# Where the gates of a mixture of experts are applied: on the combined outputs, or on the output tiles before they leave

## The chip, the cores and the metric

One core of a Trainium2 chip runs the kernel. The metric is the device time of one execution in microseconds (us); lower is better. TensorE (PE) multiplies, VectorE (DVE), ScalarE (ACT) and GpSimd (POOL) do the element work, SyncE (SP) issues most transfers. On-chip memory is SBUF; products land in PSUM, which has 8 banks (`PS[0]` to `PS[7]`).

## The reference

Three layers on 2,048 tokens of 128 numbers: a mixture of experts, a Mamba block (the mixer), and the same mixture of experts again.

```
x = x + 0.5 * moe(layernorm(x));  x = x + mamba(layernorm(x));  x = x + 0.5 * moe(layernorm(x))

moe: logits = xt @ Wr + br                      # 8 experts
     top 2 of 8 per token; gate = softmax over these two logits
     h = relu(xt @ W1[e] + b1[e])               # 128 -> 512
     y = h @ W2[e] + b2[e]                      # 512 -> 128
     out = sum over the token's two experts of gate * y
```

All is float32. Every token has two gates, with the factor 0.5 of the layer in them.

## The kernel before, in words

**Layout.** The 2,048 tokens lie as 16 tiles of 128 (`X`, 128 partitions x 16 x 128), in four groups of four tiles (the batches). Each token goes to two experts, so there are 4,096 pairs (token, choice), which fill 4,096 slots, sorted by expert: 32 tiles of 128 slots (`DENSE`). Since an expert's slots need not end with a tile, the experts work in 39 steps (`SLOT_TILES`), each on 128 slots from a computed start.

**The route** (`route`, VectorE, L1373 to L1442). From the two best logits of each token come the slot of each pair, and from the slot a pair of one-hot matrices: `onehot_a` (which tile) and `onehot_b` (which place in it, 32 blocks of 128x128 in 16-bit floats). 32 small products (L764) of `onehot_b` and `onehot_a` with the pair's number give for each slot the row to read and to write (`rows_in`, `rows_out`). `b_wide` is a helper for `onehot_b`, written by ScalarE, and free afterwards. Last in the route, VectorE works out the gates of each token (L1440 to L1442).

**The experts** (39 steps, an order written out by hand for each engine). GpSimd gathers 32 tiles of normed rows from memory (`XG`, a ring of 8: gather i waits until tile i-8 is turned), then scatters 32 tiles of outputs (`YS`, a ring of 12) to `y_rows`. It works in order, so the first scatter stands behind the last gather. TensorE at step s: first products `up(s+1)` (L793, 4 fp32 products, 8 passes, W1 x tile), transposes of arriving tiles (L778), transposes of output tiles that leave (L814), then second products `down(s)` (L805, 8 passes). VectorE at step s: half of the relu of s+1 (L1465), the copy of arrived tiles out of PSUM to `XT_all` (L1454), bias of step s (`add_bias`, L1475, into `YT_all`), and the copy of the second weights of step s+3 (`W2B`, L1484); the first three such copies stand ahead of step -2. ScalarE: the other half of the relu (L1121), copies of the first weights (`W1B`, L1111), and the copies of leaving output tiles out of bank 6 into the ring `YS` (L1133, two tiles in one instruction).

**The join.** When all scatters have landed, SyncE loads the outputs group by group (L370): for each token its two rows, `Y1` and `Y2`. Then X += gate1 * Y1 + gate2 * Y2. VectorE does it in one instruction for a tile and choice (L1507). After the first layer groups 1, 2 and part of 3 are done by ScalarE, which multiplies by the gate (`gated`, L1153), and GpSimd, which adds (L497); after the second, group 3 is. Statistics, square roots (on GpSimd, L501) and the normed rows `XN` of the mixer follow: group 0 and 3 by VectorE (`norm`, L1338), groups 1 and 2 by ScalarE (`apply`, L1000); TensorE waits for each group's rows in `time_project`.

What sets the order is each engine's own list, and semaphores; `wait_ge` stops an engine and all that is behind it on its list.

Of the kernel before, what the change touches and what calls it, by code (L numbers as in the profile page):

```python
# [14 lines left out]
P = 128  # L15
# [63 lines left out]
TURN_AT = (1, 2, 5, 3, 4)  # L79
LEAVE_STEP = [tiles[-1] + NE for tiles in LEAVES]  # L80
# [22 lines left out]
def macaron_block(nc, x, in_proj_w, conv_w, conv_b, dt_bias, A_log, D_skip, norm_w, out_proj_w,  # L103
                  ln_w, ln_b, Wr, br, W1, b1, W2, b2, out):
    ctx = ExitStack()
    with ctx:
# [66 lines left out]
        gate = sb("gate", [P, KTOP, NT])  # L173
# [20 lines left out]
        b_wide = sb("b_wide", [P, NG, P], F16)  # L194
        rows_out = sb("rows_out", [P, DENSE], I32)
# [110 lines left out]
        s_gated = sem("s_gated")  # L306
# [50 lines left out]
        def wait_xn(engine, g):  # L357

            if g in (1, 2):
                engine.wait_ge(s_xn[1], NT + g * NC)  # L360
            else:
                engine.wait_ge(s_xn[0], NC * (1 if g == 0 else 2))
# [11 lines left out]
        def _(sp_):  # L374
# [29 lines left out]
            for g in range(BATCH):  # L404
                if g < BATCH - 1:
                    sp_.wait_ge(s_comb, 2 + g + 1)
                else:
                    sp_.wait_ge(s_comb_pool, 4)
# [18 lines left out]
        def _(pool):  # L427
# [66 lines left out]
            def add_output(k, g_, gated):  # L494
                xb = X[:, g_ * NC:(g_ + 1) * NC, :]
                pool.wait_ge(s_gated, gated)
# [23 lines left out]

            def join_last():
                st.link(add_output(0, 3, 6))
                add_output(1, 3, 7).then_inc(s_comb_pool, 1)
# [116 lines left out]
            join_last()  # L640

        @block.tensor
        def _(pe):
# [109 lines left out]
            def experts(layer):  # L753
# [55 lines left out]
                def leave(m):  # L809
                    pe.wait_ge(s_ytw, B0 + min(LEAVES[m][-1] + NE, SLOT_TILES))  # L810
                    if L0 + m:
                        pe.wait_ge(s_ysc, L0 + m)
                    for k, i in enumerate(LEAVES[m]):
# [3 lines left out]

                for step in range(-2, SLOT_TILES):
                    if 0 <= step + 1 < SLOT_TILES:
# [174 lines left out]
        def _(act):  # L994
# [8 lines left out]
            def store(n, g):  # L1003
                act.wait_ge(s_xn[1], (n // 2) * (NT + 2 * NC) + (g + 1) * NC)
# [20 lines left out]
            def time_project(besides):  # L1025
                act.wait_ge(s_xnd, 16 * BATCH)
                turned(1, 0)
                besides(0)
                besides(1)
                act.wait_ge(s_rs, 2)  # L1030
                apply(1, range(NC, 2 * NC))
                turned(1, 1)
                act.wait_ge(s_rs, 3)
# [781 lines left out]
```

## Time and profile before

| | |
|---|---|
| median of 3 runs | 417.07 us (416.44 to 419.63) |
| profiled execution | 421.09 us |
| its span, first to last instruction | 419.3 us |
| TensorE busy | 330.8 us (79%) |
| VectorE busy | 269.0 us (64%) |
| ScalarE busy | 209.8 us (50%) |
| GpSimd busy | 220.7 us (53%) |

A profile is one execution with the hardware profiler on. PE is TensorE's multiplying, PEld its loading of weights; L793 is line 793 of the kernel. PEclk is the clock granted to TensorE, as a share of the full one. A row "idle before" says how long the engine stood still and whose work ended that. Starts of matmuls that follow each other are partly modelled: when TensorE is really slower than the record, one sees it only from the engines that wait for its results.

### The profile page before, as it was taken

The page shows a single profiled execution, that of the slowest core. Times are in us where ns is not written, and L with a number is a line of the kernel's source. Part 1 is how long each engine was busy: PE and PEld are TensorE (multiplying, and loading weights), DVE is VectorE, ACT ScalarE, POOL GpSimd, SP SyncE. Part 2 cuts the span into 40 slices and gives each one's busy share as a digit, 9 for nine tenths or more (in the row PEclk, how much of TensorE's full clock was granted, in tenths as well). Part 3 has the DMA queues.
Part 4 walks back from the last instruction along what each step waited for, and adds up shares of the span by engine and source line. Part 5 has one row for each costly group of instructions (what it writes and reads, how often), then busy time and mean ns, then how long its engine had stood idle before and what let it go on. Part 6 is the DMA issues. An engine that isn't in the chain of part 4 may idle for free.

```text
span 419.3 us, 8909 instructions
## 1 busy us (share of the span) xinstructions
PE 330.8 (79%) x2366; PEld 294.6 (70%) x2366; DVE 269.0 (64%) x920; ACT 209.8 (50%) x501; POOL 220.7 (53%) x263
## 2 busy tenths in 40 slices
PE   8784799986698198799999999749469998778800
PEld 7684799976697185567777779739459998767700
DVE  4883477753465178768788986899447775345416
ACT  3832456644464065736657573453245665455402
POOL 4026355566545177274656879651644556654512
PEclk9578899999899598899999999877899999899965
DMA  6791111111111410000000000010111111111154
GB/s 161 239 283 45 27 39 42 40 44 44 41 33 33 172 48 2 1 0 2 1 2 3 0 0 2 2 74 28 52 31 39 38 41 45 41 40 38 33 172 147
DMA packets 18674, 22.23 MB, mean 53 GB/s; under 512 B 4114, under 2 KB 13508, under 8 KB 18628
## 3 DMA queue, kind: packets, MB, share of 16 engines
q1 hardware_dynamic: 13092, 11.18, 8.9%
q0 software_dynamic: 4096, 8.40, 6.7%
q10 hardware_dynamic: 1440, 2.11, 1.4%
q8 instruction: 21, 0.34, 0.4%
q14 instruction: 25, 0.20, 0.2%
HBM read 14.33 MB, written 7.34 MB: 52 GB/s over the span
## 4 chain that ended last, share of the span: by engine, by line
PE 51%; DVE 11%; issue 9%; DMA 6%; SPq 6%; ACT 5%; POOL 4%; another core or an unknown queue 3%; DVEq 3%; ACTq 0%; POOLq 0%
PE PS L793 16%; PE PS L805 16%; SPq L401 3%; PE PS L842 3%; PE PS L849 3%; PE PS L896 2%; PE PS L814 2%; PE PS L778 2%; DMA YT_all<-y_rows 2%; SPq L395 2%; DMA y_rows<-YS,rows_out 2%; DVE X L1507 2%; POOL rs L501 2%; DVE YT_all L1475 1%
## 5 line engine op out<-in xcount | busy, mean ns | idle before, releaser
L479 POOL DMA_INDIRECT XG<-xn_rows,rows_in x64 | 62.1, 970 | 83.8 <-issue 35.7
L793 PE MATMUL PS<-XT_all,W1B 128*128 x624 | 90.1, 290 | 15.8 <-DVE XT_all L1454 8.0
L793 PEld LDWEIGHTS PS<-XT_all,W1B 128*128 128x128 f32 x624 | 80.3, 201 | 18.9 <-issue 18.2
L1121 ACT ACTIVATE H<-PS,W1B 128x128 f32<-128x128 f32 x156 | 48.7, 363 | 88.9 <-PE PS L793 60.7
L489 POOL DMA_INDIRECT y_rows<-YS,rows_out x64 | 62.3, 974 | 48.3 <-issue 18.9
L805 PE MATMUL PS<-H,W2B 128*128 128x128 f32 x624 | 85.3, 281 | 0.5 <-issue 0.5
L805 PEld LDWEIGHTS PS<-H,W2B 128*128 128x128 f32 x624 | 78.4, 197 | 0.9 <-issue 0.6
L1484 DVE COPY W2B<-W2S 128x513 f32 x78 | 35.5, 455 | 39.1 <-DVE YT_all L1475 26.6
L1111 ACT ACTIVATE W1B<-W1S 128x516 f32 x78 | 49.4, 633 | 21.7 <-issue 9.0
L1475 DVE TENSOR_SCALAR YT_all<-PS,W2B 128x128 f32 x78 | 27.2, 349 | 43.3 <-PE PS L805 25.8
L1465 DVE TENSOR_SCALAR H<-PS,W1B 128x128 f32<-128x128 f32 x156 | 46.9, 342 | 6.4 <-PE PS L793 3.8
L650 PE MATMUL PS<-ones 128*128 128x128 f32 x236 | 38.8, 338 | 9.7 <-DMA YT_all<-y_rows 8.6
L650 PEld LDWEIGHTS PS<-ones 128*128 128x128 f32 x236 | 37.5, 251 | 10.4 <-DMA YT_all<-y_rows 8.8
L1637 DVE SCALAR_TENSOR_TENSOR XT_all<-PS,cw,XT_all 128x509 f32<-128x509 f32 (+2 forms) x48 | 35.6, 744 | 3.9 <-ACT XT_all L1165 2.5
L814 PE MATMUL PS<-ident,YT_all 128*128 128x128 f32 x64 | 13.8, 286 | 20.3 <-DVE YT_all L1475 14.8
L540 POOL TENSOR_TENSOR mix<-eseg,gm 128x512 f32<-128x512 f32 x16 | 20.3, 1269 | 14.3 <-DVE gm L1659 14.3
L842 PE MATMUL PS<-XNT,WT 128*128 128x512 f32 x48 | 25.9, 630 | 0.3 <-ACT XNT L1010 0.3
L1507 DVE SCALAR_TENSOR_TENSOR X<-YT_all,gate,X 128x128 f32<-128x128 f32 x36 | 12.7, 419 | 19.2 <-DMA YT_all<-y_rows 19.1
L814 PEld LDWEIGHTS PS<-ident,YT_all 128*128 128x128 f32 x64 | 7.5, 141 | 23.2 <-DVE YT_all L1475 16.8
L1183 ACT ACTIVATE eseg<-PS 128x512 f32<-128x512 f32 x16 | 9.6, 597 | 26.4 <-PE PS L849 26.4
L531 POOL TENSOR_TENSOR seg_rhs<-upto,la 128x512 f32<-128x512 f32 x16 | 16.6, 1039 | 11.4 <-DVE la L1543 7.2
L1153 ACT ACTIVATE YT_all<-YT_all,gate 128x128 f32<-128x128 f32 x28 | 8.4, 388 | 22.5 <-DMA YT_all<-y_rows 22.5
(204 smaller groups left out, 556.0 us busy)
## 6 DMA issues: line engine op xcount, KB each, us to landing
YT_all<-y_rows SPq DMA_DIRECT2D x8, 512.0 KB, 5.1
W1S<-in_L_ffn_W SPq DMA_DIRECT2D x1, 2048.0 KB
W2S<-in_L_ffn_W SPq DMA_DIRECT2D x8, 256.0 KB
xn_rows<-XN ACTq DMA_DIRECT2D x8, 256.0 KB, 4.4
X<-in_L_attn_x SPq DMA_DIRECT2D x4, 256.0 KB, 4.7
XG<-xn_rows,rows_in POOLq DMA_INDIRECT x64
y_rows<-YS,rows_out POOLq DMA_INDIRECT x64
out_x<-X SPq DMA_DIRECT2D x4, 256.0 KB, 2.3
```

What stands on the lines that cost most here:

```text
L479: g.indirect_dma_start(out=XG[:, u, :], out_offset=None, in_=xn_dram, in_offset=bass.IndirectOffsetOnAxis(ap=rows_in[:, i:i + 1], axis=0), ...
L489: g.indirect_dma_start(out=y_dram, in_=YS[:, u, :], in_offset=None, out_offset=bass.IndirectOffsetOnAxis(ap=rows_out[:, i:i + 1], axis=0), ...
L650: mm(PS[bank][:, 0:P], ones[:], ones[:], start=True, stop=True)
L793: last = mm(PS[2 + 2 * half + j % 2][:, c * P:(c + 1) * P], W1B[w][:, h * P:(h + 1) * P], XT_all[:, ds(start, P)], start=True, stop=True)
L805: last = mm(PS[1 + 6 * (j % 2)][:, 0:P], W2B[w][:, c * D:(c + 1) * D], H[w][:, c, :], start=(c == 0), stop=(c == HC - 1))
L842: mm(project_bank(n, m)[:], WT[:, w0:w0 + P], XNT[:, ds(n * SEQ, SEQ)], start=True, stop=True).then_inc(s_proj, 1)
L1111: A(W1B[w][:], W1S[:, ds(e, 1), :].rearrange("p a h -> p (a h)"), ACT.Copy).then_inc(s_w1, 1)
L1121: last = A(H[w][:, 2 + c, :], PS[4 + j % 2][:, c * P:(c + 1) * P], ACT.Relu, bias=W1B[w][:, HID + 2 + c:HID + 3 + c])
L1465: last = v.tensor_scalar(H[w][:, c, :], PS[2 + j % 2][:, c * P:(c + 1) * P], W1B[w][:, HID + c:HID + c + 1], 0.0, ALU.add, ALU.max)
L1475: v.tensor_scalar(YT_all[:, ds(start, P)], PS[1 + 6 * (j % 2)][:, 0:P], W2B[w][:, HC * D:W2W], None, ALU.add).then_inc(s_ytw, 1)
L1484: v.tensor_copy(W2B[w][:], W2S[:, ds(e, 1), :].rearrange("p a d -> p (a d)")).then_inc(s_w2, 1)
L1637: last = v.scalar_tensor_tensor(out=acc[m][:, back:SEQ], in0=PS[m % 2][:, 0:SEQ - back], scalar=cw[:, BLOCKS[m], j:j + 1], in1=acc[m][:, b ...
```

## The change

The gates are no longer applied to the loaded outputs but to the output tiles, when ScalarE copies them out of PSUM. For that each slot must know its gate. VectorE works out the two gates of each token in step 1 of the experts and splits each, a 32-bit number, in three 16-bit (bfloat16) parts, taking each time the upper half of the number's bits and subtracting it. In steps 2, 3 and 4 one part each is multiplied into the one-hot matrix of tiles (`gate_a`, which lies in `b_wide`). At the head of step 6 TensorE multiplies the 32 blocks of `onehot_b`, read as bfloat16 (a one becomes 1/128, so the gates are made 128 times larger), by it, in one bank, and VectorE adds the three parts up: `gate_slot`, a number for each slot. ScalarE then scales each output tile with it, one instruction a tile.

Both ends become additions of four tiles at once, X += Y1 and X += Y2, all by VectorE, apart from three that GpSimd does after the first layer. ScalarE writes the normed rows of groups 0, 1 and 2, VectorE those of group 3. And the second weights of steps 0, 1 and 2 are copied in steps -2, -1 and 0, behind the copy of the arriving tile.

```diff
-        gate = sb("gate", [P, KTOP, NT])
+        gate = sb("gate", [P, 3, NG])
+        gate_slot = sb("gate_slot", [P, DENSE])
+        in_tile = b_wide[:, 0:NG // 4, :].rearrange("p a b -> p (a b)").rearrange("p (i q) -> p i q", q=NG)
+        gate_a = b_wide[:, NG // 4:NG, :].rearrange("p a b -> p (a b)").bitcast(BF16).rearrange(
+            "p (j i q) -> p j i q", j=3, q=NG)
...
             def join_first():
-                st.link(add_output(0, 1, 1))
-                add_output(1, 1, 2).then_inc(s_comb_pool, 1)
+                st.link(add_output(0, 2, 0))
                 root0(0)
-                wait_xn(pool, 0)
-                st.link(add_output(0, 2, 3))
-                add_output(1, 2, 4).then_inc(s_comb_pool, 1)
+                add_output(1, 2, 0).then_inc(s_comb_pool, 1)
                 root0(1)
-                pool.wait_ge(s_comb, 2)
-                add_output(1, 3, 5).then_inc(s_comb_pool, 1)
+                pool.wait_ge(s_comb, 3)
+                add_output(1, 3, 0).then_inc(s_comb_pool, 1)
                 root0(2)
                 root0(3)
...
+                def gate_columns():
+                    pe.wait_ge(s_ga, layer + 1)
+                    for q in range(NG):
+                        last = mm(PS[6][:, 0:3 * DENSE].rearrange("p (j i) -> p j i", j=3),
+                                  onehot_b[:, q, :].bitcast(BF16), gate_a[:, :, :, q],
+                                  start=(q == 0), stop=(q == NG - 1))
+                    last.then_inc(s_gcol, 1)
+
                 for step in range(-2, SLOT_TILES):
+                    if step == GATE_STEP:
+                        gate_columns()
...
                 act.wait_ge(s_xnd, 16 * BATCH)
+                act.wait_ge(s_rs, 2)
+                apply(1, range(0, NC))
                 turned(1, 0)
...
-                    A(YS[:, u:u + n, :].rearrange("p t d -> p (t d)"), PS[6][:, 0:n * P],
-                      ACT.Copy).then_inc(s_ysc, 1)
+                    if m == 0:
+                        act.wait_ge(s_gslot, layer + 1)
+                    for k, i in enumerate(tiles):
+                        last = A(YS[:, i % YS_RING, :], PS[6][:, k * P:(k + 1) * P], ACT.Copy,
+                                 scale=gate_slot[:, i:i + 1])
...
-            gated(0, 1, 0)
...
-                dve.wait_ge(s_ge, layer + 1)
-                st.link(v.tensor_scalar(gr[:], ge[:], 2.0, 2.0, ALU.mult, ALU.add))
-                st.link(v.reciprocal(gate[:, 0, :], gr[:]))
-                st.link(v.tensor_tensor(gate[:, 1, :], gate[:, 0, :], ge[:], ALU.mult))
...
+                def gates():
+
+                    dve.wait_ge(s_ge, layer + 1)
+                    st.link(v.tensor_scalar(gr[:], ge[:], 2.0 / P, 2.0 / P, ALU.mult, ALU.add))
+                    st.link(v.reciprocal(gate[:, 0, 0:NT], gr[:]))
+                    st.link(v.tensor_tensor(gate[:, 0, NT:NG], gate[:, 0, 0:NT], ge[:], ALU.mult))
+                    for j in range(2):
+                        st.link(v.tensor_tensor(gate[:, j + 1, :], gate[:, j, :], upper(j), ALU.subtract))
+
+                def upper(j):
+                    return gate[:, j, :].bitcast(BF16).rearrange("p (q h) -> p q h", h=2)[:, :, 1]
+
+                def gate_piece(j):
+                    if j == 2:
+                        side.settle()
+                    last = v.tensor_tensor(gate_a[:, j, :, :], in_tile,
+                                           upper(j).unsqueeze(1).broadcast_to([P, DENSE, NG]), ALU.mult)
...
+                def gates_by_slot():
+                    dve.wait_ge(s_gcol, layer + 1)
+                    v.tensor_reduce(gate_slot[:], PS[6][:, 0:3 * DENSE].rearrange("p (j i) -> p i j", j=3), AX.X,
+                                    ALU.add).then_inc(s_gslot, 1)
...
-                for j in range(TRIO):
-                    second_weights_of(j)
                 for step in range(-2, SLOT_TILES):
...
-                        if step + TRIO < SLOT_TILES:
-                            second_weights_of(step + TRIO)
+                    if step < 1:
+                        second_weights_of(step + 2)
+                    if 0 <= step and step + TRIO < SLOT_TILES:
+                        second_weights_of(step + TRIO)
+                    if step == 1:
+                        gates()
+                    elif 2 <= step < GATE_STEP - 1:
+                        gate_piece(step - 2)
+                    elif step == GATE_STEP:
+                        gates_by_slot()
...
-                for t in range(g * NC, (g + 1) * NC):
-                    last = add_choice(1, Y2, t)
-                last.then_inc(s_comb, 1)
+                dve.wait_ge(s_yl[g], 16 * (layer + 1))
+                st.link(add_choice(0, g))
+                add_choice(1, g).then_inc(s_comb, 1)
...
+            def add_choice(k, g):
+                xb = X[:, g * NC:(g + 1) * NC, :]
+                return v.tensor_tensor(xb, xb, (Y1, Y2)[k][:, g * NC:(g + 1) * NC, :], ALU.add)
...
             combine(0, 0)
             input_statistics(0)
-            first_choice(0, 3)
-            side.settle()
-            dve.sem_inc(s_comb, 1)
-            norm(0)
+            combine(0, 1)
             input_statistics(1)
+            input_shift(0)
+            dve.wait_ge(s_yl[3], 16)
+            add_choice(0, 3).then_inc(s_comb, 1)
             input_statistics(2)
```

The order on VectorE between the route's last result (`start_i`) and the first relu, in each layer, before (TENSOR_LOAD and ISA read a register from SBUF):

```order
L1437 TENSOR_SCALAR start_i<-start_f 128x39
L1440 TENSOR_SCALAR gr<-ge 128x16
L1441 RECIPROCAL gate<-gr 128x16
L1442 TENSOR_TENSOR gate<-gate,ge 128x16
L1480 TENSOR_LOAD te_i
L1480 ISA x2
L1484 ISA
L1484 COPY W2B<-W2S 128x513
...
L1454 COPY XT_all<-PS 128x128
L1465 TENSOR_SCALAR H<-PS,W1B 128x128 x2
```

The same place with the change:

```order
L1436 TENSOR_SCALAR start_i<-start_f 128x39
L1448 COPY XT_all<-PS 128x128
L1501 TENSOR_LOAD te_i
L1501 ISA x2
L1505 ISA
L1505 COPY W2B<-W2S 128x513
L1459 TENSOR_SCALAR H<-PS,W1B 128x128 x2
```

The gates and three second-weight copies stood ahead of the first tile's copy to `XT_all` (the line of dots stands for two more such copies); now it comes first. The order on TensorE around step 6 with the change (L801 is `down`, L789 `up`, L774 the transposes of arriving tiles):

```order
L789 MATMUL PS<-XT_all,W1B 128x128 x4
L774 MATMUL PS<-ident,XG 128x128 x2
L801 MATMUL PS<-H,W2B 128x128 x4
L819 MATMUL PS<-b_wide,onehot_b 128x96 x32
L780 TENSOR_LOAD start_i
L780 ISA x2
L789 ISA
```

Before, the row with the 32 products wasn't there, and `down(5)` was followed at once by `up(7)`. And on VectorE in step 2 (steps 3 and 4 alike):

```order
L1496 TENSOR_SCALAR YT_all<-PS,W2B 128x128
L1501 TENSOR_LOAD te_i
L1501 ISA x2
L1505 ISA
L1505 COPY W2B<-W2S 128x513
L1478 TENSOR_TENSOR b_wide<-b_wide,gate 128x1024
L1459 TENSOR_SCALAR H<-PS,W1B 128x128 x2
L1448 COPY XT_all<-PS 128x128
```

The piece of 1,024 elements (L1478) is new; the relu and the next tile's copy now stand behind it.

## Rows read from the trace of the kernel before

**Rows 1.** The chain that ended last: share of the span by engine.

```profile
...
PE 51%; DVE 11%; issue 9%; DMA 6%; SPq 6%; ACT 5%; POOL 4%; another core or an unknown queue 3%; DVEq 3%; ACTq 0%; POOLq 0%
...
```

**Rows 2.** Busy time by stretch: us, each engine busy (instructions), PEclk, DMA share, GB/s.

```profile
...
57.00:88.00 31.00, 31.00 (x278) 30.78 (x276) 22.61 (x70) 20.46 (x51) 17.50 (x19) 1.00 0.15 43
88.00:112.00 24.00, 14.52 (x117) 13.63 (x116) 9.24 (x29) 9.69 (x26) 15.15 (x16) 0.98 0.14 45
...
```

**Rows 3.** Busy time by stretch, around the starts of both experts phases.

```profile
...
36.00:40.00 4.00, 3.54 (x20) 3.14 (x19) 1.39 (x5) 0.62 (x2) 2.75 (x3) 0.58 0.19 49
...
298.00:302.00 4.00, 2.98 (x13) 2.60 (x14) 1.32 (x5) 0.62 (x2) 2.84 (x3) 0.60 0.17 51
...
310.00:314.00 4.00, 4.00 (x34) 3.82 (x34) 2.56 (x10) 2.11 (x6) 1.55 (x2) 1.00 0.06 16
...
```

**Rows 4.** Timeline, second layer: start, us, engine, line, operation, count [idle before, releaser].

```profile
...
293.64 2.09 ACT L1111 ACTIVATE W1B<-W1S 128x516 f32 x3 [5.42 <-DVE te_i L1431]
...
294.66 0.30 PE L778 MATMUL PS<-ident,XG 128*128 128x128 f32 x1 [1.07 <-DMA XG<-xn_rows,rows_in]
...
298.15 0.27 DVE L1454 COPY XT_all<-PS 128x128 f32<-128x128 f32 x1
...
298.56 1.89 PE L793 MATMUL PS<-XT_all,W1B 128*128 x8 [3.60 <-issue]
...
301.12 1.66 PE L793 MATMUL PS<-XT_all,W1B 128*128 x8 [0.46 <-issue]
...
304.62 0.62 ACT L1121 ACTIVATE H<-PS,W1B 128x128 f32<-128x128 f32 x2 [3.52 <-remote]
...
309.96 1.15 PE L793 MATMUL PS<-XT_all,W1B 128*128 x8 [2.73 <-DVE XT_all L1454]
...
312.26 0.35 DVE L1475 TENSOR_SCALAR YT_all<-PS,W2B 128x128 f32 x1 [0.71 <-PE PS L805]
...
```

**Rows 5.** Timeline, first layer, the same places.

```profile
...
23.65 1.17 PE L764 MATMUL PS<-onehot_a,onehot_b 128*128 128x32 f16 x16 [0.32 <-DVE onehot_b L1414]
...
32.59 1.92 ACT L1111 ACTIVATE W1B<-W1S 128x516 f32 x3 [8.22 <-issue]
...
34.71 0.28 DVE L1454 COPY XT_all<-PS 128x128 f32<-128x128 f32 x1
...
35.13 1.35 PE L793 MATMUL PS<-XT_all,W1B 128*128 x8 [2.85 <-DVE XT_all L1454]
...
37.16 2.07 PE L793 MATMUL PS<-XT_all,W1B 128*128 x8 [0.46 <-issue]
...
50.09 0.35 DVE L1475 TENSOR_SCALAR YT_all<-PS,W2B 128x128 f32 x1 [1.32 <-PE PS L805]
...
```

**Rows 6.** Groups by line and form: count, busy us, mean ns, idle before.

```profile
...
L489 POOL DMA_INDIRECT y_rows<-YS,rows_out x64 | 62.3, 974 | 48.3 <-issue 18.9 <-ACT YS L1133 17.9 <-DMA y_rows<-YS,rows_out 11.4
...
L1637 DVE SCALAR_TENSOR_TENSOR XT_all<-PS,cw,XT_all 128x509 f32<-128x509 f32 x16 | 11.9, 742 | 3.1 <-ACT XT_all L1165 2.5
...
L1414 DVE TENSOR_TENSOR onehot_b<-iota_n,b_wide 128x1024 f16<-128x1024 f16 x6 | 4.0, 686 | 0.0
...
L1414 DVE TENSOR_TENSOR onehot_b<-iota_n,b_f 128x1024 f16<-128x1024 f16 x2 | 2.4, 1218 | 0.0
...
L1441 DVE RECIPROCAL gate<-gr 128x16 f32<-128x16 f32 x2 | 0.5, 252 | 0.1
...
```

**Rows 7.** Timeline between the layers.

```profile
...
144.81 2.32 DVE L1507 SCALAR_TENSOR_TENSOR X<-YT_all,gate,X 128x128 f32<-128x128 f32 x8 [8.66 <-DMA YT_all<-y_rows]
...
151.37 1.12 DVE L1338 TENSOR_SCALAR XN<-X,mv,rs 128x128 f32<-128x128 f32 x4 [0.47 <-POOL rs L501]
...
157.81 1.65 ACT L1000 ACTIVATE XN<-X,shift,rs 128x128 f32<-128x128 f32 x4 [0.17 <-DVE shift L1370]
...
```

**Rows 8.** Timeline, the end of the second layer.

```profile
...
406.95 8.73 DVE L1507 SCALAR_TENSOR_TENSOR X<-YT_all,gate,X 128x128 f32<-128x128 f32 x24 [9.78 <-DMA YT_all<-y_rows]
...
410.81 2.44 ACT L1153 ACTIVATE YT_all<-YT_all,gate 128x128 f32<-128x128 f32 x8 [12.94 <-DMA YT_all<-y_rows]
...
```

More of the change, by code:

```diff
@@ L357, in wait_xn @@
         def wait_xn(engine, g):
-            if g in (1, 2):
-                engine.wait_ge(s_xn[1], NT + g * NC)
+            if g < BATCH - 1:
+                engine.wait_ge(s_xn[1], NT + (g + 1) * NC)
             else:
-                engine.wait_ge(s_xn[0], NC * (1 if g == 0 else 2))
+                engine.wait_ge(s_xn[0], NC)
         def load_outputs(engine, layer, groups):
@@ L404, in _ @@
             for g in range(BATCH):
[L405 to L408, printed above, removed]
+                sp_.wait_ge(s_comb, 3 + g + 1)
                 sp_.dma_start(of[:, g * NC:(g + 1) * NC, :], X[:, g * NC:(g + 1) * NC, :]).then_inc(s_out, 16)
@@ L492, in experts, with add_output @@
                                              ).then_inc(s_sc[u], 16)
-            def add_output(k, g_, gated):
+            def add_output(k, g_, layer):
                 xb = X[:, g_ * NC:(g_ + 1) * NC, :]
-                pool.wait_ge(s_gated, gated)
+                pool.wait_ge(s_yl[g_], 16 * (layer + 1))
                 return g.tensor_tensor(xb, xb, (Y1, Y2)[k][:, g_ * NC:(g_ + 1) * NC, :], ALU.add)
@@ L810, in leave @@
                     pe.wait_ge(s_ytw, B0 + min(LEAVES[m][-1] + NE, SLOT_TILES))
-                    if L0 + m:
+                    if m:
                         pe.wait_ge(s_ysc, L0 + m)
+                    else:
+                        pe.wait_ge(s_gslot, layer + 1)
                     for k, i in enumerate(LEAVES[m]):
@@ L1131, in copy_out @@
                             act.wait_ge(s_sc[u], 16 * (layer * ring_uses(u, YS_RING) + i // YS_RING))
-                    u, n = tiles[0] % YS_RING, len(tiles)
-                    A(YS[:, u:u + n, :].rearrange("p t d -> p (t d)"), PS[6][:, 0:n * P],
-                      ACT.Copy).then_inc(s_ysc, 1)
+                    if m == 0:
[3 more added lines that the diff above has]
+                                 scale=gate_slot[:, i:i + 1])
+                        if k < len(tiles) - 1:
+                            st.done(last)
+                    last.then_inc(s_ysc, 1)
                 for j in range(TRIO):
@@ L1147, in experts @@
                     copy_out(m)
-            def gated(layer, g, k):
-                act.wait_ge(s_yl[g], 16 * (layer + 1))
-                Yk = (Y1, Y2)[k]
-                for t in range(g * NC, (g + 1) * NC):
-                    last = A(Yk[:, t, :], Yk[:, t, :], ACT.Copy, scale=gate[:, k, t:t + 1])
-                    if t < (g + 1) * NC - 1:
-                        st.done(last)
-                last.then_inc(s_gated, 1)
             def mixer():
@@ L1467, in relu @@
                     last.then_inc(s_ra, 1)
+                def gates():
[12 more added lines that the diff above has]
+                                           upper(j).unsqueeze(1).broadcast_to([P, DENSE, NG]), ALU.mult)
+                    if j < 2:
+                        side.done(last)
+                    else:
+                        last.then_inc(s_ga, 1)
+                def gates_by_slot():
+                    dve.wait_ge(s_gcol, layer + 1)
+                    v.tensor_reduce(gate_slot[:], PS[6][:, 0:3 * DENSE].rearrange("p (j i) -> p i j", j=3), AX.X,
+                                    ALU.add).then_inc(s_gslot, 1)
                 def add_bias(j):
@@ L1788, in _ @@
             experts(1)
-            for g in range(BATCH - 1):
+            for g in range(BATCH):
                 combine(1, g)
```

42 lines of the change are left out of this document (13 added, 29 removed).

## The prediction

> **What bounds the kernel now.** I read the chain that ended last first, then the stages, then single stretches. By the chain, TensorE carries 51% of the span, VectorE 11% [rows 1]. The stage table says where: in the steady part of each experts phase TensorE is busy all the time, 278 passes in 31.00 us, 0.112 us a pass, so that one step (16 passes and one to four transposes) takes about 2.0 us, while VectorE is busy 0.73 of it [rows 2]. VectorE is thus the second bound, with some 0.5 us free in a step. Then comes a stretch of 24 us in which every engine has gaps though no engine is full and no transfer stream is (DMA share 0.14) [rows 2]; its cause I can't read. Each phase also starts badly: in the second layer the first tile of tokens is turned by 294.96, but the first up products start at 298.56, since the copy of that tile out of PSUM stands behind three copies of second weights on VectorE [rows 4]; in the first layer the same copy comes at 34.71 [rows 5]. TensorE's clock is granted at half, 0.58 and 0.60, just after these waits of 2.85 and 3.60 us [rows 3 to 5].
>
> Of the two layers' ends, the last one is bare: the loaded outputs are combined on VectorE from 406.95 to 415.68, the last group's loads land at 410.81, and nothing else is left but stores, which end with the span, 3.6 us behind the last addition [rows 8]. The first layer's end feeds the mixer through the first normed group, written 151.37 to 152.49 [rows 7].
>
> **The change, part by part.** All against the profiled execution, 421.09 us with a span of 419.3; the median of the runs shown, 417.07, is 1.0% below it, and I carry the difference over to it.
>
> *Start of the experts.* The copy of the first tile now stands ahead of the second weights' copies. What is then last is, in the first layer, the first W1B copy, 32.59 + 0.63 = 33.2; up products at 33.3 for 35.13: -1.8 us. In the second layer the W1B copy is done at 294.3 and the turned tile at 294.96; a copy of 0.27 gives 295.25, and with 0.25 of waits 295.5 for 298.56: -3.0 us. The three gate instructions that left the route are in this number.
>
> *Clock.* The gaps that preceded the half clock shrink to about 1.0 and 0.5 us, and a gap of 2.73 us ahead of 309.96 was followed by the full clock [rows 3, 4]. So I expect no fall here. The first two up groups took 1.35 + 2.07 and 1.89 + 1.66 us; 16 passes of 0.112 with 0.2 for each group's tail are 2.2: -1.2 and -1.3 us.
>
> *VectorE in steps 1 to 4.* Added are five small operations, linked, in step 1, at 0.25 and less each [rows 6], 1.3 us; and in steps 2, 3 and 4 a product of 1,024 elements. The nearest rows are 0.686 us, where both operands are read in a row, and 1.218 us, where one is spread over its inner dimension [rows 6]. The gate's upper halves are read at every second 16-bit place, so I take 1.22, with 0.69 as the other end: 3.7 us, 5.0 in all. Behind them wait the next relu and the next tile's copy, and for those TensorE. Before, VectorE had 1.32 us free there in the first layer, and 0.71 in the second [rows 4, 5]. What is left is +3.7 and +4.3 us.
>
> *The 32 products in step 6.* They bring 128x96 each. No row has this form. One end is 73 ns, 16 in 1.17 us with 32 columns [rows 5]; the other 112 ns, a pass of 128 columns [rows 2]. In between by columns: 98 ns, 3.1 us in all; ends 2.3 and 3.6. TensorE waits for the third VectorE piece first, and the next up products would have had to wait for the relu and the copy behind that piece anyhow, 0.6 + 0.4 us; so +2.1 us in each layer. The page TensorE: Matmul & The Clock Gate (Part 2, step by step) of the Trainium skill says that the next weights load while a product runs; then a product would cost only its longer half, about 56 ns, 1.8 us in all, and the forecast would be 2.6 us less. The rows speak against it here: a pass of 128 columns takes 112 ns.
>
> *Reduce and scaled copies.* VectorE's reduce of 96 elements is 0.3 us in a step with 0.5 free. ScalarE copies a pair of output tiles in two instructions instead of one, about 0.25 us more in every second step; it is busy 0.66 of the steady stretch [rows 2]. Both cost nothing, hidden behind TensorE; without that cover, 14 pairs would cost 3.5 us a layer.
>
> *Does the delay reach the phase's end?* GpSimd's gathers wait for tiles that TensorE has turned, so they move with it, and the scatters behind them. Over both layers GpSimd's scatters wait 17.9 us for ScalarE's copies [rows 6], so behind its backlog GpSimd is the faster and gives nothing back. I pass it in full. Layer one: -1.8 - 1.2 + 3.7 + 2.1 = +2.8; layer two: -3.0 - 1.3 + 4.3 + 2.1 = +2.1 us.
>
> *Between the layers.* Two wide additions and their link are 1.45 us where eight of the old took 2.32 [rows 7]: a 128x512 addition is 0.70 us, between 0.61, half of the 1.218 for 1,024 elements, and 0.742 for 509 out of PSUM [rows 6]. Group 0 is then ready 0.9 us earlier, but its rows are now normed by ScalarE (four in 1.65 us, rows of 157.81) instead of VectorE (1.12), and its shift is queued behind the additions and statistics of group 1. I get 152.15 against 152.49 for the normed group. For the later groups the shifts come earlier (157.81 was waiting for one), but TensorE's projections stand between: -0.5 us.
>
> *The end.* Landings stay: group 0 at 406.95, group 3 at 410.81 [rows 8]. Four times 1.47 us from 406.95 gives 412.8 for 415.68: -2.9 us. ScalarE's and GpSimd's shares of the last group go.
>
> **Sum:** +2.8 + 2.1 - 0.5 - 2.9 = +1.5 us; 422.6 for the profiled one, 418.6 for the median. This kernel's runs tell 1% from no change, 4.2 us.
>
> **Rivals.**
>
> (1) *The late stretch goes with the clock, faster.* After the slow first groups, ScalarE's relu waits 3.52 us more at 304.62 and TensorE 2.73 us before 309.96 [rows 4]: the second and third step took 8.8 us instead of 4. If TensorE is really slow there as an after-effect of the fall, a start without a gap saves another 4 us in each layer: 418.6 - 8 = 410.6. For it: the same stretch follows the same fall in both layers. Against it: a slow stretch with a granted clock of 0.98 stands in rows 2 as well, ahead of which nothing had idled.
>
> (2) *The vector-bound steps starve TensorE, slower.* Steps 1 to 5 would then take some 3.3 us with 2.0 us of products, and TensorE waits for the third piece. If a gap at step 6 comes to those of 2.85 us and more, the clock is halved just for the 32 products: 98 ns becomes about 190, +3.0 us, and the gain of 1.25 at the start is lost too: +4.2 a layer, 427. It decides from the point where the wait for the third piece passes 2.8 us; I work it out as under 1 us, since down products of step 5 fill it. Without the clock, but with products of 112 ns and no overlap, it is 422.
>
> (3) *The pieces are cheap.* At 0.69 us each, 1.6 us less in a layer: 415.4. With the cheap products as well, 413.8.
>
> (4) *GpSimd is the bound, so nothing of the delay shows.* If the long stretch [rows 2] is due to the scatters and not to TensorE's steps, and they don't start later, +4.9 goes: 413.7. Against: gathers wait for TensorE's transposes.
>
> (5) *It doesn't do what it says:* the ends do not shrink, since the loads land later. Then +2.9: 421.5.
>
> **Numbers.** Forecast case 0.45 (its own range 414.5 to 422.5), rival 1 0.15, rival 2 0.13, rival 3 0.12, rival 4 0.07, rival 5 0.08. Faster by over 1% (below 412.9): rival 1, a third of rivals 3 and 4, a little of the forecast's lower tail: 0.25. Slower by over 1% (over 421.2): rival 2, half of 5, a fifth of the forecast case: 0.27. Within 1%: 0.48. Leaving out the ends of rivals 1 and 2 gives 411.0 to 424.5.
>
> **What would show it.** Right: the first up products 0.5 to 1 us behind the first turned tile in each layer, and a granted clock near 1.00 there; VectorE with little idle in steps 2 to 5 and steps of 3 us; the products of step 6 about 3 us long; a span of 13 us from the last load's issue to the end, for 16.1. Wrong: pieces of 0.7 us; the products behind a long gap, or 6 us long; a late stretch that is gone, or one that has grown; a phase whose end has not moved with its step 7.

## The result, and the profile after

The changed kernel took 433.03 us (431.54 to 435.20, 6 runs), the kernel before 416.82 us beside it: 1.0383 times as long, 95% interval 1.0345 to 1.0420. Forecast were 418.6 us and no change. The profiled execution took 433.25 us with a span of 431.4 us, against 419.3 us. The two traces differ by 12.1 us, the medians by 16.2, because before's traced execution was 4.3 us above its median and the changed one's 0.2. A second trace of before, 420.76 us, lies as high above its comparison's median of 416.56, so no trace shows before at 416.5 us, and where those 4 us lie I can't tell.

The time of before depends on more than the kernel. It was 416.4 to 420.2 us in four comparisons, and 402.5 and 403.5 us in two; one chip showed both, so this isn't a kind of chip, as the expectations below call it, but a condition. I call them L (long) and S (short), give ratios within a comparison, and "us of before" is that ratio's share of its time.

**Where the time went in the two traces.** GpSimd issues the 32 gathers of a layer and then its 32 scatters, in one queue. The rows are the first gather, the last one and the first scatter of the second layer, before:

```profile
...
291.72 1.20 POOL L479 DMA_INDIRECT XG<-xn_rows,rows_in  x1 [12.52 <-issue]
...
345.67 0.94 POOL L479 DMA_INDIRECT XG<-xn_rows,rows_in  x1 [0.75 <-issue]
347.40 1.00 POOL L489 DMA_INDIRECT y_rows<-YS,rows_out  x1 [0.78 <-issue]
...
```

And after:

```profile
...
297.54 1.20 POOL L483 DMA_INDIRECT XG<-xn_rows,rows_in  x1 [12.59 <-issue]
...
362.64 0.95 POOL L483 DMA_INDIRECT XG<-xn_rows,rows_in  x1 [0.75 <-issue]
364.37 1.06 POOL L493 DMA_INDIRECT y_rows<-YS,rows_out  x1 [0.78 <-issue]
...
```

The gathers took 54.0 us and now 65.1 (first layer: 54.9 and 62.5), and the scatters follow 1.7 us behind the last gather in all of these. That is +11.1 and +7.6 us. From first to last scatter 1.3 us less go by in both layers together, from the last scatter to the next layer's first gather 0.7 less, from the last scatter to the end 14.6 us for 18.7, and the first gather is 0.5 earlier: 7.6 + 11.1 - 1.3 - 0.7 - 4.1 - 0.5 = 12.1.

The place itself, the products of step 6 in the first layer (start, us, engine, line):

```profile
...
53.16 1.22 DVE L1478 TENSOR_TENSOR b_wide<-b_wide,gate 128x1024 bf16<-128x1024 f16 x1
...
57.46 5.39 PE L819 MATMUL PS<-b_wide,onehot_b 128*128 128x96 bf16 x32
...
62.68 1.69 PE L789 MATMUL PS<-XT_all,W1B 128*128 x8
64.16 1.91 PE L801 MATMUL PS<-H,W2B 128*128 128x128 f32 x8
65.87 1.29 PE L789 MATMUL PS<-XT_all,W1B 128*128 x8
...
67.65 0.95 POOL L483 DMA_INDIRECT XG<-xn_rows,rows_in  x1 [7.30 <-PE PS L774]
...
```

One product follows another every 164 ns, where 98 was forecast; then 8 passes take 1.3 to 1.9 us for about 1.1; and GpSimd stood still for 7.30 us until TensorE had turned a tile. The stretches (us, each engine busy, PEclk, DMA share, GB/s), the first two to set beside [rows 2]:

```profile
...
57.00:88.00 31.00, 31.00 (x250) 29.34 (x249) 18.55 (x59) 16.86 (x44) 13.55 (x14) 0.94 0.11 31
88.00:112.00 24.00, 20.91 (x175) 19.66 (x173) 12.98 (x39) 13.67 (x37) 15.52 (x16) 1.00 0.15 46
...
62.70:67.00 4.30, 4.30 (x26) 4.30 (x25) 0.96 (x3) 1.26 (x3) 0.00 (x0) 0.60 0.00 0
...
329.00:331.60 2.60, 2.60 (x18) 1.81 (x17) 1.25 (x4) 0.36 (x1) 1.71 (x2) 1.00 0.17 50
331.60:334.30 2.70, 2.70 (x18) 2.04 (x17) 0.00 (x0) 0.00 (x0) 0.18 (x1) 0.68 0.09 24
...
```

TensorE is busy throughout by the record and does less: 250 passes in 31 us, 32 of them short, for 278. From 88 to 112 us it does 175 for 117, which makes up a part; yet the last gather comes at 89.98 us for 82.90. Behind the products the granted clock was 0.60 on average of its two levels, 1.2 and 2.4 GHz (0.50 from 63.5 to 66 us), though TensorE hadn't waited since 0.61 us at 55.36. The last two rows are the products of the second layer: the clock fell on the way, and their spacing, 163 ns on average, didn't change for it.

The starts, first layer, then second, to set beside [rows 5] and [rows 4]:

```profile
...
34.04 1.15 PE L789 MATMUL PS<-XT_all,W1B 128*128 x8 [1.19 <-DVE XT_all L1448]
35.77 2.07 PE L789 MATMUL PS<-XT_all,W1B 128*128 x8 [0.46 <-issue]
42.13 1.80 PE L789 MATMUL PS<-XT_all,W1B 128*128 x8 [2.66 <-DVE XT_all L1448]
45.64 1.17 PE L789 MATMUL PS<-XT_all,W1B 128*128 x8
...
```

```profile
...
301.57 1.15 PE L789 MATMUL PS<-XT_all,W1B 128*128 x8 [0.76 <-DVE XT_all L1448]
...
304.73 0.63 ACT L1131 ACTIVATE H<-PS,W1B 128x128 f32<-128x128 f32 x2 [3.17 <-remote]
...
305.19 2.00 PE L789 MATMUL PS<-XT_all,W1B 128*128 x8 [2.35 <-issue]
310.91 1.15 PE L789 MATMUL PS<-XT_all,W1B 128*128 x8 [1.94 <-issue]
316.41 2.07 PE L789 MATMUL PS<-XT_all,W1B 128*128 x8 [2.59 <-DVE XT_all L1448]
...
```

In the first layer the lead of 1.1 us is gone by the third group (42.13 for 41.95), and at the fourth it is 0.5 (45.64 for 46.16), which is what the layer's first gather was early. In the second, with the layer 5.8 us late at its first gather, the first group is 3.0 us late, so 2.8 of lead, and the fourth 6.45: none. The clock fell in both (2.07 us a group). The end, to set beside [rows 8]:

```profile
...
416.84 0.97 POOL L493 DMA_INDIRECT y_rows<-YS,rows_out  x1 [0.76 <-DMA y_rows<-YS,rows_out]
419.42 1.74 SPq L377 DMA_DIRECT2D YT_all<-y_rows  x4
423.15 5.57 DVE L1533 TENSOR_TENSOR X<-X,YT_all 128x512 f32<-128x512 f32 x8 [9.23 <-DMA YT_all<-y_rows]
424.60 4.52 SPq L413 DMA_DIRECT2D out_x<-X  x4
...
```

Eight additions in 5.57 us, where 5.9 were forecast.

### The profile page after: what moved, and what is told of

Its sections match the earlier page's. It is cut to its first block and busy times, and to the rows that moved or that the text cites. A ratio compares the mean times of both kernels' runs of the same rounds, so it can differ in the third digit from the quotient of the medians.

```text
span 431.4 us, 9023 instructions
## 1 busy us (share of the span) xinstructions
PE 352.8 (82%) x2430; PEld 313.3 (73%) x2430; DVE 275.0 (64%) x906; ACT 210.1 (49%) x505; POOL 218.0 (51%) x259
## 5 line engine op out<-in xcount | busy, mean ns | idle before, releaser
L789 PE MATMUL PS<-XT_all,W1B 128*128 x624 | 93.8, 298 | 16.3 <-DVE XT_all L1448 10.2
L789 PEld LDWEIGHTS PS<-XT_all,W1B 128*128 128x128 f32 x624 | 84.1, 209 | 20.4 <-issue 19.4
L801 PE MATMUL PS<-H,W2B 128*128 128x128 f32 x624 | 90.9, 293 | 1.4 <-issue 1.4
L801 PEld LDWEIGHTS PS<-H,W2B 128*128 128x128 f32 x624 | 84.1, 209 | 2.0 <-issue 1.9
L646 PE MATMUL PS<-ones 128*128 128x128 f32 x236 | 40.7, 350 | 9.6 <-DMA YT_all<-y_rows 8.6
L646 PEld LDWEIGHTS PS<-ones 128*128 128x128 f32 x236 | 39.4, 263 | 10.3 <-DMA YT_all<-y_rows 8.8
L1008 ACT ACTIVATE XN<-X,shift,rs 128x128 f32<-128x128 f32 x44 | 17.6, 481 | 17.3 <-DVE shift L1369 17.3
L850 PE MATMUL PS<-XNT,WT 128*128 128x512 f32 x48 | 24.9, 607 | 0.2 <-ACT XNT L1018 0.2
L1145 ACT ACTIVATE YS<-PS,gate_slot 128x128 f32<-128x128 f32 x64 | 20.0, 357 | 3.8 <-PE PS L812 2.2
L1533 DVE TENSOR_TENSOR X<-X,YT_all 128x512 f32<-128x512 f32 x13 | 9.8, 768 | 18.1 <-DMA YT_all<-y_rows 17.9
```

Of the source, the lines that this page charges most:

```text
L646: mm(PS[bank][:, 0:P], ones[:], ones[:], start=True, stop=True)
L789: last = mm(PS[2 + 2 * half + j % 2][:, c * P:(c + 1) * P], W1B[w][:, h * P:(h + 1) * P], XT_all[:, ds(start, P)], start=True, stop=True)
L801: last = mm(PS[1 + 6 * (j % 2)][:, 0:P], W2B[w][:, c * D:(c + 1) * D], H[w][:, c, :], start=(c == 0), stop=(c == HC - 1))
L850: mm(project_bank(n, m)[:], WT[:, w0:w0 + P], XNT[:, ds(n * SEQ, SEQ)], start=True, stop=True).then_inc(s_proj, 1)
```

## The experiments

| kernel | condition | time, before, us | ratio, 95% |
|---|---|---|---|
| changed, again three times | L | 434.45, 434.73, 435.84 (416.56, 416.38, 420.19) | 1.041, 1.045, 1.042 |
| products alone | L | 428.49 (416.56) | 1.0314 (1.0241 to 1.0386) |
| no gates | L | 417.72 (416.38) | 1.0020 (0.9988 to 1.0051) |
| no gates | S | 398.78 (402.50) | 0.9901 (0.9862 to 0.9940) |
| pieces alone | S | 402.24 (402.50) | 0.9987 (0.9958 to 1.0017) |
| products' columns side by side | L | 427.06 (416.38) | 1.0242 (1.0205 to 1.0279) |
| the same | S | 404.92 (402.50) | 1.0058 (1.0022 to 1.0095) |
| order alone | S | 401.61 (402.50) | 0.9980 (0.9955 to 1.0005) |
| order alone, again | S | 402.58 (403.54) | 0.9986 (0.9961 to 1.0010) |
| no gates, old order | S | 399.70 (403.54) | 0.9908 (0.9884 to 0.9933) |
| no gates, one copy a pair | S | 399.38 (403.54) | 0.9891 (0.9860 to 0.9923) |
| quarters, products at the head of step 8 | L | 427.50 (416.56) | 1.0253 (1.0201 to 1.0305) |
| quarters, products behind `up` | L | 421.34 (416.38) | 1.0131 (1.0080 to 1.0181) |
| the same, old order | L | 420.67 (420.19) | 1.0003 (0.9950 to 1.0057) |
| the same, old order | S | 401.37 (403.54) | 0.9944 (0.9919 to 0.9969) |

**Why a product takes 164 ns.** The columns of one product lie 64 bytes apart; this puts them in three runs of 32 (the piece on VectorE is written in the same order):

```diff
-            "p (j i q) -> p j i q", j=3, q=NG)
+            "p (j q i) -> p j q i", j=3, q=NG)
...
-                                  onehot_b[:, q, :].bitcast(BF16), gate_a[:, :, :, q],
+                                  onehot_b[:, q, :].bitcast(BF16), gate_a[:, :, q, :],
```

> The changed kernel, with the gates' operand of the 32 products stored so that a product's 96 columns lie in three runs of 32 neighbours instead of 64 bytes apart; nothing else differs and the output is the same. Theory A, the read of the spread operand sets the 164 ns of a product: a product falls to 70 to 110 ns, the group from 5.3 to 2.2 to 3.5 us, TensorE's clock no longer falls behind it, and the whole is 425 us (433.0 less twice 2.3 for the products and twice 1.8 for the half clock). Theory B, the price goes by the number of columns or by the weights' load: 164 ns and 433 us as before. The VectorE pieces stay at 1.22 us by both, or the permuted read of the indicator makes them dearer, up to 1.6 us.

> The changed kernel with the products' 96 columns side by side. On a chip of the faster kind 404.9 us again. On one of the slower kind: theory A, 434.5 - 2 x (5.3 - 1.5) - 2 x 1.8 of half clock, + 2 x 1.0 for the pieces of 1.90 us in place of 1.22: 425 us. Rival D, gaps of VectorE's making bring the clock down anyway: 430 us.

The piece and the products in the trace of condition S:

```profile
...
53.85 1.91 DVE L1478 TENSOR_TENSOR b_wide<-b_wide,gate 128x1024 bf16<-128x1024 f16 x1
...
55.82 1.53 PE L819 MATMUL PS<-b_wide,onehot_b 128*128 128x96 bf16 x32 [0.38 <-DVE b_wide L1478]
...
```

```profile
...
57.40:61.00 3.60, 3.60 (x32) 3.60 (x33) 1.65 (x7) 1.88 (x5) 1.09 (x2) 1.00 0.10 30
...
```

Theory A holds, beyond what it expected: 43 ns a product, the same 96 columns and weights, and the clock stays full behind them; theory B falls. In L the clock stayed full behind them too:

```profile
...
63.00:66.00 3.00, 3.00 (x29) 3.00 (x29) 1.94 (x7) 2.10 (x5) 0.95 (x1) 1.00 0.10 27
...
```

There it took 1.8% less than the change (427.06 for 434.73 us in one comparison), although each piece, which now reads its indicators 64 bytes apart, rose from 1.22 to 1.90 us, more than the 1.6 allowed for; 425 was expected by theory A, 430 by rival D. The rule I had weighed, of the Trainium skill (TensorE: Matmul & The Clock Gate, Part 2), that the next weights load meanwhile, agrees with these products, each with weights of its own; the 56 ns that I had drawn from it are too much even so, for 43 were measured, and 29 further down. Another page, which I had not drawn on, has a rule that fits: in SBUF — State Buffer (Door 1) the Trainium skill says that reads run at full rate while they stay in one 16-byte line, 8 numbers of 16 bits, and that each step to another line costs; here neighbours were 32 numbers apart. The two layouts agree with it. That the layout sets the price is shown; that the line does isn't, since no run has a distance in between.

**What is lost without the gates, with the products alone, with the pieces alone.**

```diff
-                    if step == GATE_STEP:
-                        gate_columns()
...
-                    dve.wait_ge(s_gcol, layer + 1)
-                    v.tensor_reduce(gate_slot[:], PS[6][:, 0:3 * DENSE].rearrange("p (j i) -> p i j", j=3), AX.X,
-                                    ALU.add).then_inc(s_gslot, 1)
+                    v.memset(gate_slot[:], 1.0).then_inc(s_gslot, 1)
...
-                    if step == 1:
-                        gates()
-                    elif 2 <= step < GATE_STEP - 1:
-                        gate_piece(step - 2)
-                    elif step == GATE_STEP:
+                    if step == GATE_STEP:
                         gates_by_slot()
```

That is the kernel without gates. "Pieces alone" keeps the five small operations and the pieces (the last hunk isn't made); "products alone" keeps the products and VectorE's wait for them (with a small write in place of the last piece).

> The changed kernel without any gate arithmetic: the five small operations, the three pieces, the 32 products and the reduce are left out and every slot is scaled by 1.0 (the output lacks the gates). Theory A, the loss sits in the pieces and the products: from the two traces the products with the clock behind them cost 7 us in each layer and the pieces 1 to 4.5, so 433.0 - 14 - 5.5 = 413.5 us. Theory C, the loss comes from the reordered start of the experts or from the scaled copies (ScalarE's two instructions a pair, 3.5 us a layer if not hidden): 420 us or more.

> The changed kernel with no gate arithmetic, pieces or products (the output lacks the gates), to be set against the one with the spread products alone (428.5 us beside 416.6). On a chip of the slower kind: theory A, products cost 7 us a layer: 428.5 - 14 = 414.5 us. Rival F, the reordered start itself loses there: in the trace of the products alone the second layer's seventh up products come 5.7 us later than before although its gathers begin only 2.2 us later, so 416 to 418 us. On a chip of the faster kind: 398.8 us again.

> The changed kernel with the 32 products as they are (operand 64 bytes apart) but without the five small operations and the three VectorE pieces; slots are scaled by 1.0 (the output lacks the gates). It is the kernel without gates, at 398.8 us beside 402.5, plus the products. Theory A, the products' read sets their price and the clock falls behind it: 5.3 us each plus 1 to 2 us of half clock, so 398.8 + 2 x 6.8 = 412 us, less what was hidden before. Rival D, the products only hurt together with the pieces ahead of them, which starve TensorE: 398.8 + 2 x 3.5 = 406 us and no fall of the clock.

> The changed kernel with the five small operations and the three VectorE pieces, but without the 32 products and the reduce; slots are scaled by 1.0 (the output lacks the gates). Theory A, products and the half clock behind them cost 7 us a layer: 433.0 - 14 = 419 us, with the clock full behind step 6. Theory D, it is the pieces that starve TensorE and bring the clock down, and the products only stand in that shadow: 426 us or more.

In L the products add 428.49 - 417.72 = 10.8 us to the kernel without gates (by the ratios 12.2; the two were in different comparisons), where theory A had 13.6 and rival D 7.0. The pieces add 434.45 - 428.49 = 6.0 us more (4.0 by the ratios, whose intervals overlap, so their size is rough). The products don't need the pieces: in the trace of the products alone nothing starves TensorE, and the clock falls all the same:

```profile
...
54.73 5.39 PE L819 MATMUL PS<-b_wide,onehot_b 128*128 128x96 bf16 x32
...
```

```profile
...
54.60:59.90 5.30, 5.30 (x35) 3.82 (x34) 1.24 (x4) 0.58 (x1) 2.39 (x3) 0.89 0.14 37
60.00:64.00 4.00, 4.00 (x28) 4.00 (x28) 1.03 (x4) 1.38 (x4) 0.00 (x0) 0.73 0.00 0
...
```

So rival D falls, and so does the prediction's rival 2: here the clock isn't lost by a gap but behind the spread products. With the pieces alone it stayed at 1.00 from 54 to 62 us. In S the pieces cost 3.5 us, for 10 us of VectorE's work. What surprised is the kernel without gates: all that is left of the change there are its gains, forecast at 10.7 us, and it took 0.2% more than before in L and 1.0% less in S. In L rival F (416 to 418 us) came true and not theory A (414.5), in its number; that the reordered start is what loses there isn't shown by it.

**Where the gains went.** The order alone, on the kernel before:

```diff
-                for j in range(TRIO):
-                    second_weights_of(j)
...
+                    if step < 1:
+                        second_weights_of(step + 2)
```

> The kernel before with one part of the change: the copies of the second weights stand behind the copy of the first turned tile. By the prediction's terms the starts gain 1.8 + 3.0 us and the clock 2.5: 416.8 - 7.3 = 409.5 us. By the trace of the changed kernel the lead of 1.1 us at the first up products of the first layer is gone by the third, so the rival expects 416.8 less 0 to 1.5 us, with the half clock still in both starts.

> The kernel before with the copies of the second weights behind the first turned tile, nothing else, again: it measured 0.998 of before on a chip where before takes 402.5 us. On a chip where before takes 416.5 us: rival F, the reordered start loses there what it wins: 416.5 to 421 us (the kernel without gates is 1.3 us slower there than before, although its end is 4 us shorter). The prediction's terms: 409 us.

> The changed kernel without gates (the output lacks them), with the three copies of second weights back ahead of the first tile's copy. Against the kernel before only the join, the end and the scaled copies differ. If the reordered start is what takes the end's gain away on the slower chips: 417.7 - 4 = 413 us there, and 399.5 us on a chip of the faster kind. If the order is worth nothing either way: 417.7 us again (398.8 on the faster kind).

> The changed kernel without gates, and ScalarE copies a pair of output tiles in one instruction again, unscaled (the output lacks the gates). Hidden behind TensorE, as predicted: 417.7 us again (398.8 on a chip of the faster kind). If ScalarE's second instruction is not hidden, up to 0.25 us for each of 28 pairs: as much as 7 us less, 411 us.

All four ran in S, so none tests the order where the forecast was made. Twice the order alone gave 0.2% and 0.1%, neither beyond doubt, though the first up products of its second layer come 4.1 us behind the first gather (6.8 before, in L). The trace of the first shows where TensorE stands still again, ahead of the up products of steps 15 and 18 in the second layer:

```profile
...
314.90 0.33 PE L778 MATMUL PS<-ident,XG 128*128 128x128 f32 x1 [0.45 <-DMA XG<-xn_rows,rows_in]
...
322.88 0.33 PE L778 MATMUL PS<-ident,XG 128*128 128x128 f32 x1 [1.26 <-DMA XG<-xn_rows,rows_in]
...
```

and on GpSimd, first layer:

```profile
...
76.24 0.94 POOL L479 DMA_INDIRECT XG<-xn_rows,rows_in  x1 [0.75 <-DMA XG<-xn_rows,rows_in]
77.93 0.94 POOL L479 DMA_INDIRECT XG<-xn_rows,rows_in  x1 [0.75 <-DMA XG<-xn_rows,rows_in]
79.67 1.16 POOL L489 DMA_INDIRECT y_rows<-YS,rows_out  x1 [0.79 <-DMA XG<-xn_rows,rows_in]
...
```

TensorE catches up with the gathers and waits for them. The first eight start 1.25 us apart; from the ninth on, where the code has GpSimd wait for a turned tile, it is mostly 1.69, 0.94 of work and a gap of 0.75, which the profile puts down to an earlier landing here and to "issue" in before's trace. At these spacings alone 32 gathers take 49.3 us from the first to the last (my estimate: 7 x 1.25 + 24 x 1.69). In the six traces of S without the products they took 49.8 to 52.4 us: without gates in the old order 51.4 and 50.7, with the order alone 50.0 and 50.5. In that queue the scatters stand behind them. So little of TensorE's lead can arrive in S: new order against old, the gathers of these traces are 0.4 to 1.6 us shorter in the first layer and at most 0.4 in the second. A delay, as in the trace of the pieces alone (52.2 and 52.4), goes through once the slack is used up.

In L this floor isn't reached. Before's gathers took 54.9 and 54.0 us, since some still waited for TensorE at its start:

```profile
...
48.72 0.94 POOL L479 DMA_INDIRECT XG<-xn_rows,rows_in  x1 [3.65 <-PE PS L778]
...
```

Without gates they took 53.8 and 54.5 there, so a gain of 1.1 and a loss of 0.6. Why the lead didn't reach them in L stays open. The scaled copies are free in S (without gates and with one copy a pair the ratio, 0.9891, lies within the interval of the one with two), as predicted. The kernel without gates in the old order was expected at 399.5 or 398.8 us and took 399.70 beside a before of 403.54, so it doesn't decide.

**A version that keeps the gains.** Gates in two parts, columns side by side, and the pieces cut in quarters of 256 elements, one a step:

```diff
+                    j, own = k // 4, slice(k % 4 * (NG // 4), (k % 4 + 1) * (NG // 4))
...
+                    last = v.tensor_tensor(gate_a[:, j, own, :], in_tile.rearrange("p i q -> p q i")[:, own, :],
+                                           upper(j)[:, own].unsqueeze(2).broadcast_to([P, NG // 4, DENSE]), ALU.mult)
```

First with the gates in step -1, the quarters in steps 0 to 7 and the products at the head of step 8; then all one step earlier and the products behind `up(9)`; then this with the old order of the second weights.

> A version meant to beat both: gates in two bf16 parts instead of three, the products' columns side by side in memory, the pieces cut into eight quarters of 256 elements, one in each of steps 0 to 7, the gates worked out in step -1 and the products in step 8. By theory A a quarter costs 0.48 us, within the 0.5 us that VectorE has free in a step, the 32 products cost 1.3 us, and nothing starves TensorE: 398.8 (without gates) + 2 x 1.8 = 402.4 us, even with the kernel before. Rival E, the start of the phase has no free time on VectorE, so that the quarters cost their full 3.8 us a layer: 410 us.

> The version in two parts and eight quarters, with the quarters one step earlier (steps -1 to 6) and the products behind the up products of step 8 instead of ahead of them, so that TensorE need not wait for the last quarter; it waited 2.4 us for it in each layer, and the clock fell behind that wait. If that wait was what it still paid: 427.5 - 2 x (2.4 + 1.5) = 420 us on a chip of the slower kind, 402 us on one of the faster kind. If the quarters themselves cost it: no more than 2 us less, 425.5 us.

> The version in two parts and eight quarters (421.3 us beside 416.4), with the copies of the second weights back ahead of the first tile's copy, so that only the gates' path, the join and the end are new. If the order costs 4 us on the slower chips: 417 us, even with the kernel before, and about 402 us on a chip of the faster kind. If not: 421 us again.

> The version in two parts and eight quarters in the old order, which took 0.9944 of before's time where that is 403.5 us. On a chip where before takes 416.5 us: 417 us if the reordered start costs 4 us there, 421 us if it costs nothing. On a chip of the faster kind: 0.994 again.

The products of the first (64 columns), in the first layer and the second:

```profile
...
63.30 1.11 PE L819 MATMUL PS<-b_wide,onehot_b 128*128 128x64 bf16 x32 [2.37 <-DVE b_wide L1478]
...
331.66 1.89 PE L819 MATMUL PS<-b_wide,onehot_b 128*128 128x64 bf16 x32 [2.63 <-DVE b_wide L1478]
...
```

29 ns a product at the full clock and 53 at the half one (0.50 granted from 331.6 to 333.5 us), so side by side the clock sets the price, and spread it doesn't. But TensorE waited 2.4 and 2.6 us for the last quarter, and a quarter took 0.58 us, not 0.48. So it took 9.8 us more than the kernel without gates in L (other comparison), near rival E's 11 and not theory A's 3.6. With the products behind `up(9)` the wait was gone, the clock stayed at 1.00 around them, and the time fell by 1.2%, nearer to the first of the two expectations: 3.6 us above the kernel without gates in the same comparison. The old order made 1.0131 to 1.0003 in L, but in another comparison; that the new order costs there is likely, and not shown. The last version is 0.6% faster than before in S (0.3 to 0.8) and even with it in L; in the same comparison the change took 435.84 us, 3.6% more.

**The condition.**

> The kernel before, unaltered, for a trace from the chip of this comparison. If the stretches of late results (39 to 46 and 88 to 112 us, 301 to 308 and 352 to 373 us in the trace shown ahead of the prediction) belong to the kernel, they are there again; if to the first chip, a group of 16 passes and its transposes stays near 2.0 us throughout and the span is near 400 us.

> The changed kernel once more, unaltered, on the chip of this comparison: the kernel before took 402.5 us beside the first four experiments and 416.8 us beside the first timing of the change, so the loss of 16 us has to be taken again before differences are made against it. If the loss belongs to the kernel: a ratio of 1.03 to 1.04 again, with 164 ns a product. If a part of it was the first chip's, whose traces have long stretches in which every engine waits: 1.02 to 1.03, since 404.92 us with the cheap products plus 3.7 us saved on each group of products, less the 2.0 us that the dearer pieces cost there, makes 410 to 412 us.

> The changed kernel once more, beside the last version. On a chip where before takes 403 us it has not been timed yet: 412 to 414 us by theory A (404.9 with the cheap products, + 2 x 3.8 for the products, + 2 x 1.8 for the half clock, - 2.0 for the cheaper pieces). On a chip where before takes 416.5 us: 434.5 us a fourth time.

The late stretches were there again in the second trace of before, from L (110 passes from 88 to 112 us), and that one is absent in all traces of S (210 or more); before itself wasn't traced in S. From 88 to 112 us, the order alone in S, beside [rows 2]:

```profile
...
88.00:112.00 24.00, 23.94 (x210) 23.45 (x209) 16.23 (x50) 17.08 (x43) 15.52 (x17) 1.00 0.15 46
...
```

210 passes for 117, at a granted clock of 1.00 for 0.98, about the same GpSimd time and DMA share. The kernel without gates was traced in both; its scatters, in L and then in S:

```profile
...
L493 POOL DMA_INDIRECT y_rows<-YS,rows_out x64 | 62.6, 978 | 48.7 <-ACT YS L1143 18.4 <-issue 17.4 <-DMA y_rows<-YS,rows_out 12.9
...
```

```profile
...
L493 POOL DMA_INDIRECT y_rows<-YS,rows_out x64 | 63.4, 991 | 37.2 <-DMA y_rows<-YS,rows_out 28.6 <-ACT YS L1143 6.1 <-issue 1.7
...
```

Its span was 415.3 and 395.9 us, and 18.5 of these 19.4 us lie in the two experts phases: 7.8 from first to last gather and 10.7 from first to last scatter, where GpSimd waited 18.4 us for ScalarE's copies instead of 6.1. What makes TensorE late in L no row shows; it stays open. The changed kernel was timed in L alone, so its loss in S isn't known.

## Why the prediction was wrong

Its sum was 12.2 us of gate work less 10.7 us of gains. Measured in L, in one comparison, were 17.0 us (434.73 - 417.72) and no gain (417.72 for 416.38). So two things failed: the gains, by some 12 us, and the price of the 32 products. By its steps:

- **Start of the experts and clock** (-1.8, -3.0, -1.2, -1.3): failed, 7.3 us. The leads appeared at the first group, 1.1 and 2.8 us, but the clock fell anyway, and none of it shows in L's medians. The failing sentence is "I pass it in full", said of a sum of delays and leads. In S the gathers' own pace is a floor under a lead, which rival 4 had named for delays. In L, where the forecast was made, that floor isn't reached, and what took the lead is open.
- **The 32 products** (+2.1 a layer): failed. 5.3 us for 3.1, and behind them the half clock, which cost some 1.6 and 2.5 us (24 passes in 4.3 and 5.2 us for 2.7), in all 5.4 to 6 us a layer by the times. I interpolated by the number of columns between rows that differ in how the operand lies. The row of 73 ns for 32 columns [rows 5] was one with columns 64 bytes apart as well: 2.3 ns a column, 5 times what the columns side by side cost (43 ns for 96).
- **VectorE in steps 1 to 4** (+3.7, +4.3): right in kind, 2.0 to 3.0 us a layer in L and 1.7 in S; the piece took 1.22 us as taken.
- **Reduce and scaled copies** (0): the copies right, in S; the reduce, 0.25 us, wasn't tested by itself.
- **Between the layers** (-0.5): -0.7 in the traces.
- **The end** (-2.9): -4.1 from the last scatter. In L the medians don't show it, since before's traces lie 4 us above theirs; in S the kernel without gates in the old order, where only the join, the end and the copies are new, is 3.8 us faster (403.54 - 399.70).

Of the rivals, 2 was the nearest in sign and time (427), and had the half clock at step 6, but by a gap that wasn't there; that its number lies near is luck. Rival 1 is refuted: in the second layer ScalarE still waited for TensorE until 304.73, though the gap ahead was 0.76 us and 1.00 was granted from 300 to 303, and with the order alone in S TensorE did 51 passes from 39 to 46 us (28 before) although 0.50 was granted from 33 to 36.

## What to carry to other kernels

Cost a product by how its moving operand lies in SBUF before counting its columns. Before counting an earlier start, look for a queue that issues at its own pace between it and the end: a lead is worth no more than the slack to it (in S at most 1.6 and 0.4 us, for 3.0 and 4.3 counted), while a delay beyond the slack goes through. Lay an operand out for whichever reader is the bound; here VectorE paid 0.7 us a piece so that TensorE saved 3.9 us a layer.

## What was not expected of the hardware

- 96 bf16 columns 64 bytes apart: 164 ns a product, at the full clock and on average across its fall; in runs of 32 side by side 43 ns; 64 such columns 29 ns, or 53 at the half clock.
- TensorE, busy by the record all along, was granted half the clock behind 5.3 us of spread products, and the full one behind 1.5 us of the same products side by side.
- A VectorE multiplication of 1,024 16-bit elements took 0.69 us with both operands in a row [rows 6], 1.22 with one at every second place, and 1.90 with the indicators read 64 bytes apart and each gate repeated. The first two fit a rule of the Trainium skill (VectorE: DVE Perf Modes, Mode 2×_1P: two results a cycle only with neighbours).
- One kernel, one chip, two comparisons: 416.4 and 403.5 us. By the two traces of the kernel without gates nearly all of such a difference lies in the experts phases.
